# Attention block and gated layer on one core: small constants on ScalarE's queue, one channel of the read weights per partition, tables inside the order, first part ordered anew

## The reference

```python
x = x + xattn(layernorm(x), pos, ctx)      # x: 2 x 512 x 1024
x = x + ffn(layernorm(x))

def layer_forward(hidden, ...):            # hidden: 256 features x 4 channels
    qkv_in = rat_read(hidden, attn_read_w, g, b, 3)     # y = einsum('blhc,hoc->bloh'), then a norm over h
    attn_out = attention(qkv_in, qkv_w, pos)            # 16 heads of 16, rotary, causal
    hidden = rat_write(hidden, attn_out, ...)           # hs * A_full + out * B_full per channel
    mlp_in = rat_read(hidden, mlp_read_w, g, b, 2)
    mlp_out = silu(g_in @ ctx[0].T) * (u_in @ ctx[1].T)
    return rat_write(hidden, mlp_out, ...)

def _binary_diff_weight(w, base):
    d = w - base
    return base + jnp.mean(jnp.abs(d)) * jnp.sign(d)    # one mean per matrix
W1, W2, W3 = ...                           # each 3584 x 1024, with a base of the same size
ffn = (silu(x @ W1.T) * (x @ W3.T)) @ W2.T
```

## Time and profile before

| | us |
|---|---|
| median of 3 runs | 1407.24 (1401.03 to 1408.16) |
| the profiled execution | 1408.62 |
| its span, first to last instruction | 1406.8 |
| TensorE busy in the span | 1292.9 (92%) |
| VectorE / ScalarE / GpSimd busy | 868.6 / 530.1 / 361.9 |

### The profile page before, as it was taken

One profiled execution on the slowest core, in us unless ns is written; L12 is line 12 of the kernel. 1 busy time (PEld: TensorE's weight loads), 2 busy tenths in 40 slices (PEclk: granted clock), 3 DMA queues, 4 the chain that ended last, 5 costly groups with the idle time before them and its releaser, 6 DMA issues.

```text
span 1406.8 us, 16747 instructions
## 1 busy us (share of the span) xinstructions
PE 1292.9 (92%) x6548; PEld 1015.8 (72%) x6548; DVE 868.6 (62%) x1135; ACT 530.1 (38%) x809; POOL 361.9 (26%) x197
## 2 busy tenths in 40 slices
PE   4887788877887899999999999999999999999998
PEld 4754555545665678888888888888788888888887
DVE  6768777778878865546564546363645546554544
ACT  4776665855655432222222222222222222222220
POOL 2222333233234422222222222222222222222210
PEclk9998988987899899999999999999999999999999
DMA  8476887577731222322222222232222232222312
GB/s 339 147 273 252 287 285 267 208 288 274 268 132 31 105 90 93 105 102 90 90 94 97 109 90 90 90 106 102 91 90 90 95 111 94 90 90 90 116 34 120
DMA packets 53826, 197.55 MB, mean 140 GB/s; under 512 B 6626, under 2 KB 6900, under 8 KB 53236
## 3 DMA queue, kind: packets, MB, share of 16 engines
q1 hardware_dynamic: 53748, 196.49, 38.7%
HBM read 192.27 MB, written 4.19 MB: 140 GB/s over the span
## 4 chain that ended last, share of the span: by engine, by line
PE 72%; DVE 15%; issue 5%; ACT 5%; DMA 2%; POOL 1%; SPq 0%; DVEq 0%; ACTq 0%
PE pair L969 42%; PE quad L1068 17%; PE pair L952 2%; DVE negwide L1372 2%; PE quad L915 1%; DMA ctxw<-in_mean_w 1%; DVE raw_w L1448 1%; DVE hid L1438 1%; PE pair L1022 1%; PE quad L905 1%; PE pair L843 1%; ACT prob L1122 1%; PE pair L824 1%; DVE wr_q L1425 1%; DVE big L1547 1%
## 5 line engine op out<-in xcount | busy, mean ns | idle before, releaser
L1633 POOL TENSOR_TENSOR raw_w<-raw_w,raw_base 128x1024 f32<-128x1024 f32 x84 | 215.5, 2567 | 661.5 <-DMA raw_base<-in_mean_w 661.5
L969 PE MATMUL pair<-xnT_hi,w_hi 128*128 128x512 f32 x880 | 343.8, 391 | 3.3 <-DVE xnT_lo L1557 3.3
L969 PE MATMUL pair<-xnT_lo,w_hi 128*128 128x512 f32 x880 | 343.6, 390 | 0.0
L969 PE MATMUL pair<-xnT_hi,w_lo 128*128 128x512 f32 x880 | 343.5, 390 | 0.0
L1590 DVE TENSOR_TENSOR hf<-sgf,pair 128x512 f32<-128x512 f32 x56 | 38.5, 688 | 282.1 <-PE pair L969 282.1
L1182 ACT ACTIVATE w_hi<-raw_w 128x1024 fp32r<-128x1024 f32 x84 | 88.8, 1058 | 324.0 <-DVE raw_w L1448 323.8
L969 PEld LDWEIGHTS pair<-xnT_hi,w_hi 128*128 128x128 f32 x880 | 166.1, 189 | 38.6 <-issue 2.7
L969 PEld LDWEIGHTS pair<-xnT_lo,w_hi 128*128 128x128 f32 x880 | 165.9, 189 | 34.5
L969 PEld LDWEIGHTS pair<-xnT_hi,w_lo 128*128 128x128 f32 x880 | 165.9, 189 | 34.4
L1068 PE MATMUL quad<-w_hi,h_hi 128*128 128x512 f32 x448 | 175.4, 391 | 9.3 <-DVE hid L1570 9.3
L1448 DVE SCALAR_TENSOR_TENSOR raw_w<-raw_w,coeff,raw_base 128x1024 f32<-128x1024 f32 x84 | 166.8, 1988 | 19.9 <-ACT raw_w L1165 19.9
(11 more groups left out here) (234 smaller groups left out, 1561.4 us busy)
## 6 DMA issues: line engine op xcount, KB each, us to landing
raw_w<-in_w SPq DMA_DIRECT2D x84, 512.0 KB, 3.8
raw_base<-in_mean_w SPq DMA_DIRECT2D x84, 512.0 KB, 4.6
part<-in_w SPq DMA_DIRECT2D x28, 512.0 KB, 4.1
part<-in_mean_w SPq DMA_DIRECT2D x28, 512.0 KB, 5.3
ctxw<-in_w SPq DMA_DIRECT2D x28, 512.0 KB, 4.8
ctxw<-in_mean_w SPq DMA_DIRECT2D x28, 512.0 KB, 6.3
big<-in_w SPq DMA_DIRECT2D x20, 512.0 KB, 3.8
big<-in_mean_w SPq DMA_DIRECT2D x20, 512.0 KB, 4.8
```

What stands on the lines that cost most here:

```text
L969: a = pe.matmul(banks[gate_bank(u, b)], ww[:, k, :], xx[:, k, :], start=k == 0 and n == 0, stop=k == KF - 1 and n == 2)
L1633: pool.tensor_tensor(w[:, :], w[:, :], base[:, :], ALU.subtract).then_inc(f_diff, 1)
```

## The change

- The five small constants are issued from ScalarE's queue; `ident` has a semaphore of its own. SP begins with x tile 0.
- Of `w_in` only each partition's channel is loaded, in four loads of 32 partitions (384 and 256 KB in all), and `diag` is one instruction over 128 partitions instead of four over 32.
- The rotary tables are three steps (`tables`) of the order, with waits where they are used; the loads of the MLP's write weights are a step too (`wr1`).
- TensorE issues 14 matmuls on `ones` into a free bank before its order.
- The order's durations, its leads, and the times at which SP's loads are taken to be there are new; single steps have leads of their own (`OWN`, 90 of them).

```diff
 MEASURER = ("DVE", "DVE", "POOL")
@@
+ISSUE, LANDING, HOP, TABLE = 0.8, 1.6, 0.05, 1.3
+AHEAD_OF = {"PE": 0.16, "DVE": 0.08, "ACT": 0.09, "POOL": 0.04, "SP": 0.0}
-    free_at = {"PE": 0.0, "DVE": 0.0, "ACT": 0.0, "POOL": 0.0, "SP": 40.0}
+    free_at = {"PE": 0.0, "DVE": 0.0, "ACT": 0.0, "POOL": 0.0, "SP": 16.0}
-MEASURE_WEIGHT, PULL = 4.89, 0.00247
-FIRST = {"back": (-2.3, -2.4, -2.9, -2.9), "coef": (-14.3, 2.9), "ctx": (14.3,), "diag": (28.9, 31.7),
+MEASURE_WEIGHT, PULL = 1.283, 0.00015
+FIRST = {"back": (-2.5, -2.5, -3, -2.8), "coef": (3.1, 1.7), "ctx": (5.8,), "diag": (40.9, 64), "early": (-28,),
+SLOW = {"PE": 1.042, "DVE": 1.156, "ACT": 1.074, "POOL": 0.964}
+WARM = 14
@@ SP
-            sp.dma_start(ident[:, :], d["ident"]).then_inc(ld_const, 16)
-            sp.dma_start(cmask, d["cmask"]).then_inc(ld_const, 16)
-            sp.dma_start(pos_i[:, :], d["pos"]).then_inc(ld_const, 16)
-            sp.dma_start(inv[:, :], d["inv_freq"]).then_inc(ld_const, 16)
-            sp.dma_start(gb[:, :, :, :], d["gb"]).then_inc(ld_const, 16)
+            def load_reads(t):
+                for c in range(C):
+                    rows = slice(32 * c, 32 * c + 32)
+                    sp.dma_start(w_in[t][rows, :, :], d[f"w_in{t}"][rows, c]).then_inc((ld_win0, ld_win1)[t], 16)
+            load_x(0)
+            load_reads(0)
+            load_x(1)
+            sp.dma_start(wqkv[:, :, :], d["wqkv"]).then_inc(ld_wqkv, 16)
+            load_x(2)
+            load_x(3)
+            load_reads(1)
+            load_x(4)
+            load_x(5)
+            load_write(0)
@@ TensorE
-            pe.wait_ge(ld_const, 80)
-            pe.wait_ge(masks, 2)
+            pe.wait_ge(c_ones, 1)
+            for k in range(WARM):
+                pe.matmul(banks[7][:, 0:P], ones[:, :], ones[:, :], start=True, stop=True)
+            pe.wait_ge(ld_ident, 16)
@@ ScalarE
+            act.dma_start(ident[:, :], d["ident"]).then_inc(ld_ident, 16)
+            act.dma_start(pos_i[:, :], d["pos"]).then_inc(ld_const, 16)
+            act.dma_start(inv[:, :], d["inv_freq"]).then_inc(ld_const, 16)
+            act.dma_start(cmask, d["cmask"]).then_inc(ld_const, 16)
+            act.dma_start(gb[:, :, :, :], d["gb"]).then_inc(ld_const, 16)
@@ VectorE
-                    dve.wait_ge((ld_win0, ld_win1)[t], 16)
-                    for c in range(C):
-                        rows = slice(32 * c, 32 * c + 32)
-                        a = dve.tensor_tensor(diag[t][rows, :, :, :], w_in[t][rows, c, :, :].rearrange("p o (k j) -> p k o j", j=32),
-                                              eye[rows, :].unsqueeze(1).unsqueeze(1).to_broadcast([32, NB, WAYS[t], 32]), ALU.mult)
-                    a.then_inc(diags, 1)
+                    dve.wait_ge((ld_win0, ld_win1)[t], 16 * C)
+                    dve.tensor_tensor(diag[t][:, :, :, :], w_in[t][:, :, :].rearrange("p o (k j) -> p k o j", j=32),
+                                      eye[:, :].unsqueeze(1).unsqueeze(1).to_broadcast([P, NB, WAYS[t], 32]), ALU.mult
+                                      ).then_inc(diags, 1)
```

219 lines of the change are left out of this document (126 added, 93 removed).

## The result

| | before | after |
|---|---|---|
| median, us | 1403.03 (1401.03 to 1408.16) | 1415.84 (1409.11 to 1424.52) |
| profiled execution, its span | 1408.62, 1406.8 | 1417.2, 1415.4 |
| ratio after/before, 95% interval | | 1.008 (1.006 to 1.0101) |

What follows compares the result with a forecast made beforehand. Before 493 us a chain of dependent steps in fixed order was taken to bound the part changed, no engine being full. Terms +6 - 8 - 3 - 3 = -8 us gave 1400.6 profiled, 1399 as median; range 1383 to 1416.

Steps and rivals of the forecast that it cites:

- the -3 of the end: End of the first part: TensorE's 6.9 us wait for inner shrinks as products precede updates; -3 us, bounds 0 to -6.9.
- the 0 of the rest: Order elsewhere, shuffled by one or two places nearly everywhere: 0 us, bound 8 us either way.
- the first term: Start, up to the first read: diag0 ends at 22.8 us instead of 16.7; +6.0 us, bounds +5.6 to +7.5.
- The first long gated run: First long run of gated matmuls, at 492.65 us before, should start at about 485 us.
- First read at 22 to 24 us: Sign at the start: first read matmul starts then, with diag0 directly ahead and VectorE's first difference at about 19 us.
- The small constants leave together from ScalarE's queue: Start: the constants issued there were to be complete at about 4.4 us, as before.
- The smaller product wins 2.9 us: Start: diag0 as one instruction takes 0.95 us instead of 3.84; its place in the order gives back 8.9.
- The start is passed on to the attention: After the first read, the tile-to-tile chain keeps its links, so the 6.0 us reach the attention.
- -8 for stalls: Fourth to eighth oT: earlier measurement loads remove engine stalls; -8 us, bounds 0 to 10.5 us of stalls.
- -3 for fewer measurements: Fourth to eighth oT: 17 measurement sums stand where 21 stood; -3 us, bounds 0 to -5.
- the start is passed on and nothing comes back: Rival for the attention: measurement only fills gaps, so the 6.0 us loss remains; 1415 us, chance 0.20.
- the gated layer stays at 914 us: From 493 us to the end: the change touches nothing there, so this layer only slides and keeps its length.

Runs made afterwards that it cites:

- a_sp_waits: Changed kernel, with SP issuing its first large load only after all five small constants have landed: 1414.19 us, ratio 1.007.
- b_compact: Kernel before, with only the one-channel loads of w_in0 and w_in1 and single-product diag0 and diag1: 1404.88 us, ratio 0.9992.
- b_all_but_order: Kernel before with one-channel loads, single diag products and small constants on ScalarE's queue, order of steps kept: 1408.74 us, ratio 1.003.
- a_consts_sp: Changed kernel with the five small constants issued from the front of SP's queue instead of ScalarE's: 1412.33 us, ratio 1.0048.
- a_diag_early: Changed kernel with diag0 and diag1 moved right behind tile 0's statistics in VectorE's list: 1410.79 us, ratio 1.0037.
- a_start: Changed kernel with diag0 and diag1 behind tile 0's statistics, constants first on SP, ScalarE's waits for them behind the sines: 1415.03 us, ratio 1.0081.
- a_head: Changed kernel, constants first on SP, ScalarE's waits behind the sines, about 50 head steps of VectorE, ScalarE, GpSimd in the old sequence: 1422.14 us, ratio 1.0132.
- b_lean: Kernel before, moving only 8 of 128 partitions of the second load of most measurement units: 1411.96 us, ratio 1.0074.
- the splices: Kernel before with one-channel loads, taking the changed kernel's sequence from the 16th oT or from behind row 7: 1398.65 and 1395.20 us.
- b_splice2: Kernel before with one-channel loads, old order up to the last step of row 7, then the changed kernel's sequence: 1395.20 us, ratio 0.993.
- b_splice8: Kernel before with one-channel loads, old order up to the 8th oT, then the changed kernel's sequence: 1416.17 us, ratio 1.0088.

## Why the prediction was wrong

The forecast was +6 - 8 - 3 - 3 + 0 = -8 us. In the two profiled executions the pieces gave +16.3 where +6 stood, -10.3 where -8 and -3 stood, -13.1 for the -3 of the end, +14.0 (4.9 and 9.1) for the 0 of the rest, and 1.7 in the gated layer: +8.6. The steps that failed are the first term and the rest put at 0. The first long gated run started at 499.5 us, not at 485.

**First read at 22 to 24 us: wrong, 31.4.** The step that failed first is "The small constants leave together from ScalarE's queue and are there at about 4.4 us as before". Moving them was treated as a matter of issue time. They landed at 9.1, and a_sp_waits shows why. The first difference started at 25.8 instead of 18.8, and 4.7 of these 7.0 us are this. The rest are waits inside VectorE's layer norms, which the prediction added up without any: 1.70 us for a tile that ScalarE normalised later, and 0.59 and 0.66 for GpSimd's power. The load of ScalarE's sine table, which "occurs as often as before" but now behind a wait, held VectorE by only 0.21 us (its wait at 13.12). Then the collision with GpSimd fell on an instruction of one column, 2.30 us for 0.15. The prediction had it as an upper bound. It ended at 30.39 us, GpSimd's difference at 30.38. The Trainium skill's rule ("SBUF — State Buffer", the shared port pair), by which the loser waits for the whole instruction, agrees with this row.

**"The smaller product wins 2.9 us": wrong.** b_compact won nothing at the first read. `xT` of tile 0 was ready within 0.1 us of `diag0`, which the prediction did not look up.

**The start is passed on to the attention: right.** 4.5 us later at the first read gave 4.0 at the 16th `oT` and 3.9 in the time (b_all_but_order against b_compact), and in a_consts_sp and a_diag_early what the second read won (3.2 and 4.3 us) is there at the 16th `oT` (3.3 and 4.1). It is not a law of this kernel: a_start and a_head lost on the way what their second read had won. And the first read alone counts for nothing, since the second has ScalarE's list ahead of it (a_diag_early).

**-8 for stalls and -3 for fewer measurements: the sign and the size came, the meaning was wrong.** The 4th to the 8th `oT` shrank by 10.3 us where 11 were forecast. ScalarE's waits for differences fell from 11.5 to 6.8 us (forecast from 10.5 to under 4), and the landings went off the chain there. But TensorE's idle time in the piece fell by only 2.0 us (18.5 to 16.5), and b_lean took every wait of VectorE for a landing away in the order of before without shortening it (83.2 us). So most of it was no stall. The work in the piece says what it was. Before (columns of the earlier trace rows):

```profile
100.00:182.70 82.70, 64.25 (x576) 39.28 (x580) 63.80 (x84) 55.32 (x98) 24.54 (x13) 0.86 0.74 264
```

After:

```profile
121.20:193.60 72.40, 55.96 (x470) 30.97 (x470) 54.52 (x68) 42.40 (x73) 20.41 (x11) 0.79 0.70 250
```

TensorE has 8.3 us less to do in it, VectorE 9.3, ScalarE 12.9. By a count of the two lists the new order has done more up to the 4th `oT` (fill 9, two steps each of the queries of tiles 4 and 5, five units of the measurement) and less up to the 8th (the second reads of tiles 0 and 1, fill and use 25 and 26). The work was moved mostly ahead: from the 1st to the 4th `oT` TensorE is busy 3.4 us longer, and up to the 1st 6.1 longer, 5.4 of them the warming. From the 8th to the 16th, where the list has steps more and others less, no engine has more than 0.5 us more to do; what that piece lost is another matter (below). The prediction counted sums only, and looked at one piece of a list without what was moved to the pieces beside it. The measurement's lead was gone early: the 13th sum came at 100.3 us (99.3 before), the last at 431.2 (404.7).

**-3 for the end: the right wait, far too small.** 13.1 us, of which the splices carry 9.7 into the order of before. The wait for `inner` went as foreseen, and there were two of them, 10.0 us. Two things stood at nothing in the sum. The collisions of the updates with GpSimd, of which one row of 2.98 us was quoted, were 8.9 us in all. And TensorE's own matmuls got shorter: 6.0 of the 13.1 us are busy time, with 24 matmuls more in the piece (7.3 of 9.7 in b_splice2, with the same number).

**The rest of the reshuffle, 0 with a bound of 8: too narrow.** Between the 8th and the 16th `oT` 9.1 us were lost, and all of it is idle time of TensorE (25.1 to 34.1 us); its busy time stayed at 116 us. It waits 11.4 us for `prob` where it waited 6.3, 7.5 for `negwide` against 3.9, and 5.6 for `big` from VectorE against 3.2. So it is not moved work but the sequence that waits more for ScalarE and VectorE, as b_splice8 says too; which places in the lists do it stays open.

**The rival** "the start is passed on and nothing comes back" had the price 1415 and the right time, with wrong parts, which is luck: more was lost at the start and between the 8th and the 16th `oT`, and more came back at the end. The last sentence, that the gated layer stays at 914 us, held (915.9).

## What to carry to other kernels

When lists are fixed beforehand, cost a moved block by every piece that it left and entered, with all engines' work and waits in each; a single piece that gets shorter is no gain until its neighbours are counted. Where TensorE waits in a busy part, look at the matmuls behind the wait too: they may run at the slow level. A second queue gave the small loads no priority over large ones beside them: issue what the first instructions wait for ahead of everything, on whatever queue. Before crediting a faster step, look at what its user waits for besides it; and before moving a step ahead in a list, look at what its own data waits for.

## What the runs showed of the hardware that was not expected

- Loads of 4 to 64 KB took 5.1 to 6.5 us from issue to landing beside another queue's large loads, and 1.7 to 1.9 us ahead of them.
- A VectorE instruction on 128 x 1 elements took 2.30 us while GpSimd worked on 128 x 1024, the same form 0.15 us alone. b_lean, with half of the measurement's bytes left out, had more such collisions and was slower.
- Sixteen products of 128 x 376 took 7.73 us at a granted clock of 0.68, 6.83 at 0.78 and 5.32 at 1.00. In b_splice2 this was worth 7.0 us of one piece.
- The granted clock from 0 to 48 us read 1.00 before and 0.68 after, but the first eight transposes took 1.94 us in both. Directly behind 10 us of warming they took 1.06 us, and the reads after 3.18 us of idleness 3.62 us.
